# A phase of its own for level zero of the triangular inversion, in a four-layer kernel that runs in two lanes

## The reference

```python
A = jnp.where(tri, 0.0, -jnp.einsum('bhncd,bhned->bhnce', kb, k))
for i in range(1, chunk):
    upd = jnp.einsum('...k,...kj->...j', A[..., i, :], A[..., :, :i])
    A = A.at[..., i, :i].add(upd)
inv = A + jnp.eye(chunk, dtype=A.dtype)
u = inv @ v
w = inv @ kb
```

## Time and profile before

| | |
|---|---|
| median of 3 runs | 6054.68 us (6027.5 to 6063.11) |
| the profiled execution's own time | 6045.51 us |
| its span, first to last instruction | 6044.2 us |
| PE busy | 4245.8 us, 70% |
| PEld busy | 3259.7 us, 54% |
| DVE busy | 2998.6 us, 50% |
| ACT busy | 1939.8 us, 32% |
| mean granted TensorE clock | 0.736 of full speed |
| first to last score matmul, layer 0 attention | 66.9 to about 970 us |
| first to last score matmul, layer 2 attention | 3022.6 to 3887.1 us |

### The profile page before, as it was taken

How to read it: one execution, slowest core, us unless ns; L and a number is a source line. 1 busy time by engine, 2 the same in 40 slices (tenths; PEclk the granted TensorE clock), 3 DMA queues, 4 the chain that set the end, 5 groups by cost and what they waited for, 6 DMA issues and landing times.

```text
span 6044.2 us, 94874 instructions
## 1 busy us (share of the span) xinstructions
PE 4245.8 (70%) x39740; PEld 3259.7 (54%) x39740; DVE 2998.6 (50%) x7965; ACT 1939.8 (32%) x4236; POOL 817.7 (14%) x600
## 2 busy tenths in 40 slices
PE   6686968468878887855475766757767677766298
PEld 5574847345555565544364655634444445445277
DVE  4445363335555555565446455455565555555333
ACT  2233132223333333311323233234444444442122
POOL 0000000231110111124200000011111111110443
PEclk6555555588888888866666666568887788778599
DMA  9100000240000000011200000000000000000255
GB/s 260 40 2 1 2 1 2 76 128 1 1 1 1 1 1 1 1 35 19 48 2 1 1 1 1 2 1 1 1 1 1 1 1 1 1 1 1 66 162 141
DMA packets 140860, 152.33 MB, mean 25 GB/s; under 512 B 7808, under 2 KB 128002, under 8 KB 139792
## 3 DMA queue, kind: packets, MB, share of 16 engines
q1 hardware_dynamic: 119024, 128.21, 7.4%
q0 software_dynamic: 21408, 18.05, 1.8%
HBM read 87.38 MB, written 59.76 MB: 24 GB/s over the span
## 4 chain that ended last, share of the span: by engine, by line
PE 50%; DVE 29%; ACT 12%; issue 4%; POOL 2%; DMA 1%; another core or an unknown queue 1%; SPq 0%; DVEq 0%; POOLq 0%; ACTq 0%
PE banks_lane L800 4%; ACT work L3226 4%; PE banks_lane L422 3%; PE banks_lane L3663 2%; PE banks_lane L1882 2%; PE banks_lane L3068 2%; PE banks_lane L1249 2%; PE banks_lane L808 2%; PE banks_lane L3112 2%; DVE weights L3319 1%; PE banks_lane L949 1%; ACT work L1976 1%; PE banks_lane L3147 1%; DVE work L2789 1%; PE banks_lane L1940 1%
## 5 line engine op out<-in xcount | busy, mean ns | idle before, releaser
L422 PE MATMUL banks_lane<-constants,work 128*128 128x128 f32 x968 | 202.2, 358 | 513.8 <-DVE work L408 231.5
L422 PEld LDWEIGHTS banks_lane<-constants,work 128*128 128x128 f32 x968 | 155.1, 186 | 587.2 <-DVE work L408 222.8
L402 POOL TENSOR_TENSOR weights<-weights,constants 128x4 f32<-128x4 f32 x76 | 78.5, 1033 | 2126.7 <-DVE weights L397 2126.7
L422 PE MATMUL banks_lane<-constants,weights 128*128 128x128 f32 x596 | 124.2, 347 | 339.1 <-DVE weights L408 99.0
L3226 ACT ACTIVATE work<-banks_lane,weights 128x192 f32<-128x192 f32 (+1 forms) x512 | 248.2, 498 | 245.8 <-DVE weights L3323 245.8
L422 PEld LDWEIGHTS banks_lane<-constants,weights 128*128 128x128 f32 x596 | 88.5, 178 | 372.2 <-issue 172.6
L3331 POOL TENSOR_TENSOR weights<-weights,constants 128x16 f32<-128x16 f32 x64 | 185.4, 2896 | 530.9 <-DVE weights L3239 530.9
L402 POOL TENSOR_TENSOR work<-work,constants 128x4 f32<-128x4 f32 x76 | 77.3, 1018 | 1199.2 <-DVE work L397 1199.2
L3147 PE MATMUL banks_lane<-constants,work 128*128 128x128 f32 x896 | 149.7, 316 | 120.0 <-DVE work L3311 70.5
L3147 PEld LDWEIGHTS banks_lane<-constants,work 128*128 128x128 f32 x896 | 113.2, 160 | 149.9 <-DVE work L3311 89.0
L2029 DVE TENSOR_REDUCE work<-banks_lane 128x2 f32<-128x512 f32 x256 | 158.9, 684 | 68.0 <-PE banks_lane L1896 67.8
(11 more groups left out here) (779 smaller groups left out, 11169.5 us busy)
## 6 DMA issues: line engine op xcount, KB each, us to landing
work<-experts_dram_l_ffn SPq DMA_DIRECT2D x39, 964.0 KB
room_l_ffn<-work SPq DMA_DIRECT2D x30, 1188.0 KB, 15.4
work<-experts_dram_l_ffn SPq DMA_DIRECT2D x23, 512.0 KB
weights<-weights_dram SPq DMA_DIRECT2D x1, 4833.5 KB, 14.0
work<-room_l_ffn SPq DMA_DIRECT2D x36, 132.0 KB, 3.3
weights<-weights_dram SPq DMA_DIRECT2D x1, 4112.0 KB, 12.8
weights<-bands_dram SPq DMA_DIRECT2D x1, 4096.0 KB, 13.1
weights<-room_l_ffn SPq DMA_DIRECT2D x26, 132.0 KB, 4.5
```

The lines of the kernel that those rows point to most:

```text
L402: pool.tensor_tensor(n.rstd, n.rstd, c("neghalf", cols=(0, n.rstd.shape[1])), ALU.pow).then_inc(*u.pool.step(name))
L422: done = pe.transpose(bank[0:rows, t * P:(t + 1) * P], block, c("ident"))
```

## The change

Phase `score` is cut in two. The scores, NT and AT stay in `score`; what DVE does for level zero becomes a phase named `strict`. On PE, ACT and POOL the new phase is empty, and ACT's copies of the diagonal blocks stay in `score`. No instruction is added, removed or altered, and no wait is added.

```diff
 def delta_phases(pair):
-    names = [f"score{pair}"]
+    names = [f"score{pair}", f"strict{pair}"]
@@ score_pe
         yield f"score{pair}"
+        yield f"strict{pair}"
@@ L0Attn.dve and L2Attn.dve
+            yield f"score{pair}"
             d.level0_dve(dve, u, pair)
-            yield f"score{pair}"
+            yield f"strict{pair}"
             yield from d.levels_dve(dve, u, pair, filters)
```

## The result

The changed kernel takes 5997.97 us (median of 6 runs, 5990.53 to 6018.32); the kernel before, over its 6 runs, 6045.72 us. The ratio is 0.9935, 95% interval 0.9918 to 0.9952: faster by 0.65%, or 39 us, in the interval 29 to 50. The two medians lie 48 us apart, inside that interval. The prediction had 43.9 us less, to 6010 us, with 5985 to 6040 as its range. Over six runs the median of before came out 9 us lower than over the three known at the time of the forecast, which is most of the 12 us between 6010 and 5998.

The account below looks back on a forecast made before the run. No engine is full, so handovers bound it: B's 16 waits for level zero's transpose, 68.6 us. Terms 4.3 + 13.6 + 26.0 = 43.9 us, from 6054.7 to about 6010 us, range 5985 to 6040.

Parts of the forecast that it names:

- The measure: At each place, an earlier start of B's first left product carries everything behind it along; 43.9 us in all.
- The signs named beforehand: B's first left product 8.6 us after layer 0's activation, 9.8 after A's AT, 13.9 after B's steps in layer 2.
- Layer 0, second pairs: B's scores, moved ahead, start at 437.2 instead of 440.61: 3.4 us at four places, 13.6 us.
- Layer 0, first pairs: B's left product starts at about 352.3 instead of 353.61, held by busy PE: 1.2 us at three places.
- The very first place: First pair of all, in layer 0: a gain of 0.7 us, between nothing and 1.2.
- part of the work runs at full clock: At the first place of all, given with B's earlier scores as reason for taking 0.7 us instead of 1.2.
- Layer 2: B's steps begin 3.2 us earlier: 2.6 us at four first pairs, 3.9 at four second pairs, 26.0 us.
- its parts 7.75 and 6.10: Layer 2: 7.75 us from B's steps to its NT and AT, 6.10 from B's NT to its left product.
- The clock behind the places: Rival: TensorE stays at 2.4 GHz for two left and two right products more per place, 37 us more, 5973; 9%.
- Nothing was given back: Judges the rival that B's earlier levels meet a hidden wait: no change, 6055, or part of the gain, 6035; 12%.
- the third rival: A's products fall onto the path, A's mask standing behind B's AT: at most 4.4 us a place, 6081; 3%.

Follow-up runs that it names:

- the second set: The unaltered changed kernel run once more against the kernel before: 0.9946 (0.9932 to 0.9961), 6002.31 us against 6037.59.
- layer 2 alone: The new phase `strict` only in the layer 2 attention, layer 0 as in the kernel before: 0.9962 (0.9950 to 0.9974), 6011.4 us.
- nt_first: The changed kernel with VectorE making layer 2's four NT ahead of the four AT instead of in turn: 0.9924 of before, 5994.07 us.
- layer 0 alone: The new phase `strict` only in the layer 0 attention, layer 2 as in the kernel before: 0.9972, 6018.58 us against 6036.05.
- the two kernels with one engine's order: Against the kernel before: TensorE's new order with level zero among the scores on VectorE, 1.0044; VectorE's new order with TensorE's old list, 1.0018.
- nt_held: nt_first with layer 0's biased activation of the held product on ScalarE moved ahead of the three key copies: 0.9920 of before, 5990.48 us.

## Why the prediction was right, step by step

- *The measure.* B's first left product as the point from which the rest follows was right: the gains of the places add to 43.4 us, the two attentions as stages lost 43.9, and the times moved by 39 (29 to 50). In the second set they moved by 33 (24 to 41), a little less than the places say. The signs named beforehand came too: B's first left product starts 8.5 us after the start of the activation in layer 0's first pairs (forecast 8.6), 9.8 after A's AT in its second pairs (9.8), and 13.7 after B's steps in layer 2 (13.9).
- *Layer 0, second pairs*, 3.4: exact. That B's scores then need only the copied output is the wait in the trace, 0.98 us for line 1200. The state was early because level zero left the phase of the scores on DVE; with level zero left among the scores it was late, and B's scores came 1.3 us sooner after A's instead of 3.4. So most of this term rests on both halves of the change, which the prediction had used without saying so.
- *Layer 0, first pairs*, 1.2 against 1.3: right, and bound by a busy TensorE as said: no idle before B's left product.
- *The very first place*, 0.7: the two profiles show -1.0. The step that failed is "part of the work runs at full clock": it took the clock for a property of the place, and it is one of the execution. The stretch from 76.5 to 83.5 us, columns as in the earlier trace rows, in the profile of before, of the change, of layer 2 alone (whose layer 0 is that of before) and of nt_first (whose layer 0 is that of the change):

```profile
76.50:83.50 7.00, 4.70 (x137) 3.98 (x136) 3.45 (x10) 4.12 (x10) 0.00 (x0) 0.99 1.24 242
```

```profile
76.50:83.50 7.00, 5.52 (x73) 4.70 (x76) 3.12 (x8) 4.12 (x10) 0.00 (x0) 0.50 1.24 247
```

```profile
76.50:83.50 7.00, 6.78 (x129) 5.88 (x130) 2.31 (x8) 2.68 (x7) 0.00 (x0) 0.50 1.24 258
```

```profile
76.50:83.50 7.00, 4.54 (x136) 3.99 (x136) 3.97 (x11) 4.12 (x10) 0.00 (x0) 0.96 1.22 265
```

Each order ran with either clock. With B's scores at full clock the place took 17.96 us before and 17.33 in nt_first, a gain of 0.6, which is the forecast; at half clock it took 20.28 (layer 2 alone) and 18.97, a gain of 1.3 as at the other first pairs. The -1.0 sets a full clock against a half one, and no run shows that the change lowers the clock: these scores took 1.17 us in two of the three profiles with TensorE's old order and in three of the six with the new one. At equal clock the places add to 45 or 46 us instead of 43.4.
- *Layer 2*, 2.6 and 3.9 against 2.7 and 4.0: right, with its parts 7.75 and 6.10 at 7.73 and 6.00. That the scores' half clock leaves the path in the second pairs shows in their equal length from steps to left product, 13.7 us in both. The fourth first pair of the change ran its scores in 2.11 us and took 18.43, like the other three at 1.17.
- *Are both halves needed?* VectorE's order alone gives nothing, which the run with TensorE's old list shows: the new work waits behind an item that waits for the other engine. For TensorE's order alone no run exists, since the kernel meant for it also put A's mask behind B's level zero on VectorE. It shows that the scores moved ahead cost time if level zero stays among them; how much they would give beside VectorE's old list is open.
- *The rivals.* The clock behind the places did not stay up: TensorE's left products of the levels take 1.92 us after the change too, and the granted clock behind the place in layer 0's second round (345 to 352 us) is 0.50. Nothing was given back: the wait list lost 53.6 us at line 891 and no later stage grew by more than 0.4 us. A's mask did not reach the path in the whole change, by 0.17 us in layer 0's first pairs; where level zero stayed among the scores it did, and the kernel became slower, which is the third rival's mechanism.
- *The scatter.* The profile of the change lost 11 us more than its places. The layer 1 attention explains 7 of it and is scatter: 1346 us before, and 1339, 1347, 1343, 1342, 1342, 1357, 1352 and 1344 us in the change, its repeat, layer 0 alone, layer 2 alone, the two kernels with one engine's order, nt_first and nt_held, all with the same code. The repeat of the change settles that it is no effect of the order.

## What to carry to other kernels

When two lanes alternate on in-order engines, look for the item that is both waiting and standing in front of the other lane's ready work, and move it behind, on every engine on which it stands there: moving it on VectorE alone only brought TensorE a wait of 3.27 us for it. When you test one engine's half, compare the other engine's list of instructions with that of before; here TensorE's half was never tested by itself, because a phase that is empty on an engine still shifts its two lanes against each other. Price such a move by the start of the last handover that everything behind follows, and count all the items that the new order puts in front of it. Then read the waits that are left: they named the next two steps (the wait of 0.96 us and that of 1.48), which brought 5990.48 us, 0.80% (0.66 to 0.93) under the kernel before.

## What was not expected of the hardware

The granted clock of TensorE differed between executions at one and the same place with the same instructions and gaps in front. In nt_first, whose layer 0 code is that of the change, the first pair of the second round ran its scores in 1.17 us and its left product in 1.27, where the change has 2.11 and 1.92:

```profile
341.32 1.17 PE L782 MATMUL banks_lane<-work 32*128 32x256 f32 x16 [1.48 <-ACT work L1184]
342.42 1.27 PE L801 MATMUL banks_lane<-weights,work 64*64 64x32 f32 x32
...
347.70 1.92 PE L801 MATMUL banks_lane<-work 64*64 64x32 f32 x32
```

The granted clock there (338 to 345 us) was 0.74 against 0.50, and the place took 17.70 us instead of 18.97. In both, TensorE had done twelve transpositions in 2.82 us and stood 1.48 us before the scores. Three of four first pairs of nt_first ran so and none of the change's or its repeat's. The kernel before does it too: with its layer 0 code B's scores at the fourth first pair took 2.11 us in one profile and 1.17 in another (layer 2 alone), with 2.82 us of transpositions and 0.23 us of idle before A's left product in both. So 1.3 to 2.3 us at one place are decided by something other than the order. What it is, no run shows: none shifted a stage by a known time. The same holds for whole stages. The layer 1 attention scatters over 18 us, and the layer 2 attention took 1019.0 us in nt_first and 1029.3 in nt_held with the same code. That bounds what a single profile can say about a change of this size: sums by places are firmer than spans, and even a place has to be compared at equal clock.
